# Attention phase of a graph kernel: flags made once, rotations for two chunks at a time, layer one moved by three DMAs a chunk, loads issued ahead

## The reference, cut to what matters

```python
        # attention, edge_index = (src, dst)
        q = (x @ Wq).reshape(N, N_HEADS, D_HEAD)
...
        scores = jnp.einsum('ehd,ehd->eh', q[dst], k[src]) * inv_sqrt_d
        m = jax.ops.segment_max(scores, dst, num_segments=N)
...
        e = jnp.exp(scores - m[dst])
        denom = jax.ops.segment_sum(e, dst, num_segments=N)
        msg = jax.ops.segment_sum(e[:, :, None] * v[src], dst, num_segments=N)
        attn_out = msg / jnp.maximum(denom, 1e-16)[:, :, None]
        out = attn_out.reshape(N, N_HEADS * D_HEAD) @ Wo
        return x + out
...
        # tensor product: 384 weights of an edge from its scalar, spherical harmonics Y of its direction
        R = jax.nn.relu(abs_distances[:, None] @ w1 + b1) @ w2 + b2
...
                    acc = acc + _NORM[i] * jnp.einsum('euv,ef,evi,ofi->euo', Rb[..., k], Yf, Fb, C)
...
        out = out.at[dst].add(msg)
        return out
...
    h = jnp.maximum(_layernorm(x, axis=-1), 0.0)
    x = x + _L0_gnn_ref(h, L0_gnn_Wq, L0_gnn_Wk, L0_gnn_Wv, L0_gnn_Wo, edge_index)
    h = jnp.maximum(_layernorm(x, axis=-1), 0.0)
    x = x + _L1_gnn_ref(h, edge_weight, edge_attr_3, edge_index, L1_gnn_w1, L1_gnn_b1, L1_gnn_w2, L1_gnn_b2)
    return x
```

## Time and profile before

| | |
|---|---|
| time, median of 3 runs | 8775.19 us (8774.19 to 8779.57) |
| profiled execution, first to last instruction | 10754.7 us |
| PE, DVE, ACT, POOL busy in it | 3832.9, 5399.1, 1875.2, 6468.4 us |
| attention loop, first to last gather | 317.7 to 4838.2 us |
| tensor-product loop, first to last gather | 5088.2 to 10541.2 us |
| largest group of instructions | L988, 3132 gathers, 3073.6 us busy |
| second | L534, 3132 gathers, 2992.4 us busy |

### The profile page before, as it was taken

One profiled execution on the slowest core, in us unless ns is written; L12 is line 12 of the kernel. 1 busy time (PEld: TensorE's weight loads), 2 busy tenths in 40 slices (PEclk: granted clock), 3 DMA queues, 4 the chain that ended last, 5 costly groups with the idle time before them and its releaser, 6 DMA issues. The chain is left out here.

```text
span 10754.7 us, 65813 instructions
## 1 busy us (share of the span) xinstructions
PE 3832.9 (36%) x15884; PEld 2560.9 (24%) x15884; DVE 5399.1 (50%) x8641; ACT 1875.2 (17%) x2288; POOL 6468.4 (60%) x6677
## 2 busy tenths in 40 slices
PE   1000000000000000000576666666766666676663
PEld 0000000000000000000344444444444444444442
DVE  3223333333433333333566666666666666666664
ACT  0123222222222222221011111111111111111110
POOL 6776666666666666664555555555555555555554
PEclk6555555555555555555788888888888888888887
DMA  6334334334333433432122222222222222222221
GB/s 244 84 85 100 102 96 100 93 95 100 99 101 92 101 92 97 103 96 55 41 49 51 50 51 52 49 48 51 53 48 49 51 49 51 52 50 52 49 51 32
DMA packets 417113, 797.24 MB, mean 74 GB/s; under 512 B 166622, under 2 KB 244174, under 8 KB 404798
## 3 DMA queue, kind: packets, MB, share of 16 engines
q1 hardware_dynamic: 152488, 491.52, 16.4%
q0 software_dynamic: 213216, 166.16, 9.5%
q10 hardware_dynamic: 51126, 136.22, 3.3%
HBM read 499.75 MB, written 293.61 MB: 74 GB/s over the span
## 5 line engine op out<-in xcount | busy, mean ns | idle before, releaser
L988 POOL DMA_INDIRECT feat<-scratch_h,src x3132 | 3073.6, 981 | 2422.4 <-issue 1006.7
L534 POOL DMA_INDIRECT kv<-scratch_kv,src_i x3132 | 2992.4, 955 | 1533.4 <-issue 965.7
L1221 DVE TENSOR_TENSOR prod<-psR,ops 128x384 f32<-128x384 f32 (+1 forms) x3132 | 1936.3, 682 | 1807.0 <-remote 1335.6
L1014 PE MATMUL psS<-prod,ident 128*128 128x288 f32 x7656 | 2091.5, 433 | 2.1 <-DVE prod L1221 2.1
L1003 PE MATMUL psR<-whigh,stack 128*128 128x384 f16 x3132 | 1127.5, 361 | 1634.7 <-DVE prod L1221 1493.0
L1014 PEld LDWEIGHTS psS<-prod,ident 128*128 128x128 f32 x7656 | 1582.8, 208 | 470.5 <-issue 28.3
L798 PE MATMUL psA<-ident,tail 128*36 128x128 f32 x3 | 0.8, 414 | 4578.3 <-DVEq L823 4578.3
L1004 PE MATMUL psR<-wlow,capped 128*128 128x384 f16 x3132 | 1131.4, 362 | 96.7 <-issue 93.6
L798 PEld LDWEIGHTS psA<-ident,tail 128*36 128x36 f32 x3 | 0.3, 128 | 4578.5 <-DVEq L823 4578.4
L1003 PEld LDWEIGHTS psR<-whigh,stack 128*128 128x128 f16 x3132 | 323.8, 103 | 2081.8 <-DVE prod L1221 1693.0
L641 DVE TENSOR_TENSOR sq<-attr 128x162 f32<-128x162 f32 x58 | 19.1, 329 | 1518.4 <-DMA attr<-in_attr 1039.8
(11 more groups left out here) (253 smaller groups left out, 4355.2 us busy)
## 6 DMA issues: line engine op xcount, KB each, us to landing
w_row<-in_wT SPq DMA_DIRECT2D x232, 432.0 KB
stack<-scratch_hid SPq DMA_DIRECT2D x174, 576.0 KB
scratch_state<-out ACTq DMA_DIRECT2D x58, 1080.0 KB
kv<-scratch_kv,src_i POOLq DMA_INDIRECT x3132
qin<-scratch_qexp SPq DMA_DIRECT2D x58, 864.0 KB
scratch_hid<-high SPq DMA_DIRECT2D x232, 216.0 KB
scratch_hid<-low SPq DMA_DIRECT2D x232, 216.0 KB
feat<-scratch_h,src POOLq DMA_INDIRECT x3132
```

The costliest lines, as they stand in the source:

```text
L534: nc.gpsimd.indirect_dma_start(kv[b][:, t, :], None, a["kv"], bass.IndirectOffsetOnAxis(ap=src_i[b][:, t:t + 1].bitcast(U32), axis=0)).the ...
L988: nc.gpsimd.indirect_dma_start(feat[h][:, t, :], None, a["h2"], bass.IndirectOffsetOnAxis(ap=src_i[b][:, h * PACK + t:h * PACK + t + 1].bi ...
L1014: nc.tensor.matmul(psS[:, 0:GC].rearrange("p (t c) -> p t c", c=COLS), ident[:, :], prod[r][:, :, j, :], start=(n == 0), stop=False)
L1221: v.tensor_tensor(to[:, :, :, lo:lo + n], psR[:, g % 2, :, frm:frm + n * JC].rearrange("p t (j u) -> p t j u", j=JC), ops[j % 2][:, ts, x ...
```

## The change: what it does

- **Flags.** All destination numbers are loaded at once (`dst_all`, 128x3132) before the loop, and one instruction makes all 58 chunks' flags, straight into the tile that `tensor_product` reads. In the loop L646, L648 and L650 go, with their loads; ScalarE makes the penalty from the flags by a scale and a bias.
- **Frames.** Directions are loaded, squared, rooted and turned for two chunks at a time (128x108 where 128x54 stood). The turning stands in the second chunk of a pair, after the split and before the wait for the gathered rows. Some instructions no longer wait for the one before.
- **Layer one.** The scalars of a chunk come by one DMA, the hidden units go out by two. `w_row`, `high` and `low` are one tile each of two pieces, where each piece was a tile with a semaphore.
- **Loads ahead.** Queries of the first two chunks are loaded ahead of the loop, then each two chunks ahead; the directions a pair ahead.
- **Counting.** DVE's count of its own instructions is cleared at the end of each pair, so its waits are for constants and the register instructions between them (L115) go.

```diff
-        dst_i = [sb(f"dst_i{b}", [P, T1], I32) for b in range(2)]
-        attr = [sb(f"attr{b}", [P, T, 3]) for b in range(2)]
+        dst_all = sb("dst_all", [P, SLOTS + 1], I32)
+        attr = sb("attr", [P, 2 * T, 3])
...
-        w_row = [sb(f"w_row{q}", [P, PIECE]) for q in range(2)]
+        w_row = sb("w_row", [P, 2 * PIECE])
+        high, low = sb("high", [P, 2 * PIECE], FP16), sb("low", [P, 2 * PIECE], FP16)
...
+                def load_w(chunk):
+                    sp.dma_start(w_row[:, :],
+                                 a["wT"][bass.ds(chunk * (T * P), T * P)].rearrange("(h o n) -> h o n", h=2, o=1).to_broadcast([2, HID, 2 * PIECE])
+                                 ).then_inc(w_here, 16)
+                def store_units(units_of, row):
+                    sp.dma_start(a["hid"][bass.ds(row, HID), :].rearrange("k (h n) -> h k n", h=2),
+                                 units_of[:, :]).then_inc(hid_stored, 16)
...
                 def body(i, last):
                     for b in range(2):
...
+                        chunk = i * 2 + b
+                        if not last:
+                            sp.wait_ge(q_free, chunk + 1)
+                            load_q(b, chunk * T + 2 * T)
+                        sp.wait_ge(split_done, chunk * 2 + 3)
+                        if not (last and b == 1):
+                            load_w(chunk + 1)
+                        store_units(high, chunk * P)
+                        store_units(low, chunk * P + HID)
+                    if not last:
+                        sp.wait_ge(attr_free, i + 1)
+                        load_attr(i * (2 * T) + 2 * T)
+                    sp.wait_ge(frame_ready, i + 1)
+                    sp.dma_start(a["frame"]..., frame[:, :, :]...).then_inc(frame_stored, 16)
...
-                        nc.scalar.activation(pen_c[:, :, :], spread_front(pen[:, :], HEADS), ACT.Copy).then_inc(spread_ready, 1)
+                        nc.scalar.activation(pen_c[:, :, :], spread_front(flags, HEADS), ACT.Copy, scale=BIG, bias=-BIG).then_inc(spread_ready, 1)
...
+                        act.wait_ge(w_here, i * 32 + b * 16 + 16)
                         for q in range(2):
...
+                            if q == 0:
+                                act.wait_ge(hid_stored, i * 64 + b * 32 + 32)
+                            nc.scalar.activation(high[:, cols], units, ACT.Copy).then_inc(high_ready, 1)
...
+                vec.wait_ge(dst_loaded, 32)
+                step(v.tensor_tensor(same[:, :, 1:T1], by_chunk(dst_all[:, 1:SLOTS + 1]), by_chunk(dst_all[:, 0:SLOTS]), ALU.is_equal))
...
+                        if b == 1:
+                            vec.wait_ge(rn_ready, i + 1)
+                            rotations(step, i)
...
+                    vec.sem_clear(vec_done)
```

More of the change, by code:

```diff
@@ L495, in _ @@
                     sp.dma_start(b1[half, :], a["b1"]).then_inc(w_loaded, 16)
-                load_w(0, 0)
-                load_w(1, 0)
+                load_q(0, 0)
+                load_attr(0)
+                load_w(0)
+                load_q(1, T)
                 def body(i, last):
                     for b in range(2):
[L501 to L520, removed]
@@ L633, in _ @@
                 own_block(vec)
                 with vec.Fori(0, PAIRS) as i:
-                    step = chain(vec, vec_done, base + i * (2 * steps))
+                    step = chain(vec, vec_done)
+                    vec.wait_ge(attr_loaded, i * 16 + 16)
+                    step(v.tensor_tensor(sq[:, :, :], attr[:, :, :], attr[:, :, :], ALU.mult))
+                    step(v.tensor_reduce(rn[:, :], sq[:, :, :], axis=AX.X, op=ALU.add))
+                    vec.sem_inc(rn_asked, 1)
                     for b in range(2):
@@ L647, in _ @@
-                        vec.sem_inc(dst_free, 1)
-                        step(v.tensor_scalar(pen[:, :], same[:, :], BIG, -BIG, ALU.mult, ALU.add))
-                        vec.sem_inc(flags_ready, 1)
-                        step(v.tensor_copy(k["same"][:, bass.ds(i * 2 + b, 1), :].rearrange("p c t -> p (c t)"), same[:, :]))
-                        vec.wait_ge(rn_ready, c1)
-                        step(v.reciprocal(rn[:, :], rn[:, :]))
-                        vec.wait_ge(frame_free, c1)
-                        fr = frame[b]
@@ L663, in _ @@
-                        step(v.tensor_tensor(inv[:, :], sgn[:, :], nz, ALU.add))
-                        step(v.reciprocal(inv[:, :], inv[:, :]))
-                        step(v.scalar_tensor_tensor(out=xy[:, :], in0=ny, scalar=-1.0, in1=inv[:, :], op0=ALU.mult, op1=ALU.mult))
-                        step(v.tensor_tensor(fr[:, :, 6], xy[:, :], nx, ALU.mult))
-                        step(v.tensor_tensor(xy[:, :], xy[:, :], ny, ALU.mult))
-                        step(v.tensor_tensor(fr[:, :, 7], xy[:, :], sgn[:, :], ALU.add))
@@ L669, in _ @@
-                        step(v.tensor_scalar(fr[:, :, 8], ny, -1.0, None, ALU.mult))
-                        step(v.scalar_tensor_tensor(out=fr[:, :, 5], in0=nx, scalar=-1.0, in1=sgn[:, :], op0=ALU.mult, op1=ALU.mult))
-                        step(v.tensor_tensor(fr[:, :, 4], fr[:, :, 6], sgn[:, :], ALU.mult))
-                        step(v.tensor_tensor(xy[:, :], nx, inv[:, :], ALU.mult))
-                        step(v.tensor_tensor(xy[:, :], xy[:, :], fr[:, :, 5], ALU.mult))
-                        step(v.tensor_scalar(fr[:, :, 3], xy[:, :], 1.0, None, ALU.add))
@@ L707, in _ @@
                         vec.sem_inc(sums_ready, 1)
-                    assert step.count[0] == 2 * steps, step.count[0]
+                    vec.sem_clear(vec_done)
                 vec.wait_ge(sums_copied, CHUNKS * 2 + 2)
```

124 lines of the change are left out of this document (64 added, 60 removed).

## The result

| | us (lowest to highest) | runs |
|---|---|---|
| before | 8774.69 (8758.42 to 8779.57) | 4 |
| after | 10,090.76 (10,079.21 to 10,092.04) | 4 |
| ratio | 1.15 [1.1483, 1.1516] | |

The account below looks back on a forecast made before the run. The prediction took POOL's gathers to bound a timed run's attention loop. All parts counted 0 except 3 us won on POOL's own pace: 8775.2 - 3 = 8772 us, no change that can be told (0.66); 8-in-10 range 8670 to 8800.

Parts of the forecast that it names:

- Layer one: Attention loop, SP's queue: 5 DMAs a chunk for 17, claimed 0 timed; a load at most 5.5 us later, cost 0.
- slack of 26.9 us: Attention loop, each chunk: POOL's gathers of 67.5 us less the 40.6 us chain of DVE and ACT, claimed to cover late loads.
- POOL paces a timed run of before: Attention loop: gathers at 1.25 us, 67.5 us a chunk, outlast the 40.6 us chain, so the change leaves the bound untouched.
- rival of a real stall in attention: Attention loop: up to 164 us of stalls are real when timed and go, giving 8611, middle 8693; chance 0.24.
- The residue: Whole timed run: 164 us left for both loops' stalls, 8775.2 less 8611.2 of outer stretches and back-to-back gathers.
- Stalls in the profile and hardly any in a timed run: Both gather loops: a timed run has at most 164 of the profile's 2143 us of stalls, 8%.
- The span of 10,190 in the profile: Profiled execution after the change: nearly all 567 us of POOL's buffer waits go, from 10754.7 to about 10190 (10150 to 10350).
- Flags, frames, loads ahead, 0 and -3 us: Attention loop: these parts gain 0 timed; fewer DVE instructions beside POOL's gathers win 3 us, bounds 0 and 25.
- Slower rival: Attention loop: the scalars' load has rows twice as long, gathers queue behind them, 46 us, giving 8821; chance 0.07.
- Faster, because DVE's steps hold gathers up: Attention loop: 25 fewer DVE steps a pair free POOL, 25 us (8750) or 196 us (8579); chance 0.03.
- DVE's idle goes to `kv`: Attention loop, changed kernel's profile: DVE idles ahead of the product with gathered keys, on `kv`'s landing, instead of before the squares.

Follow-up runs that it names:

- both undone: Changed kernel with its joined load made two DMAs and its two stores four, of 64 partitions each: 8793.21 us, 1.002 of before; 0.9846 on a slower chip.

## Why the prediction was wrong

The step that failed is *Layer one*: "One load is now later by what the first piece had ahead, 5.5 us at most ... Cost 0". It priced the joined DMA by the issue it saves and took its transfer at the pace that the rows of before showed for DMAs of 64 partitions. None of the rows that it read was of a DMA led by 2. The transfer's length should have been an unknown with bounds, the upper one for rows two at a time instead of sixteen. Where the prediction had the load 5.5 us later, its rows take 38.3 us and the stores' another 36.1 behind them. The wait that carries the loss in one chunk of a pair was named ("ACT's first fp16 copy of a chunk waits for all stores of the last one"); the one of the other chunk, DVE's for the directions behind the stores on SP's queue, was not. The slack of 26.9 us was the wrong measure, too: one joined set of 36 to 38 us exceeds it and costs 2.9 or 11.6 us in the whole kernel, because it runs beside DVE's and ACT's work. What counts is the turn from one load to the next. It exceeds the gathers by 88.2 - 67.5 = 20.6 us a chunk, and 58 of these are the 1195.7 (67.5 is 3917.8 / 58).

Point by point:
- *POOL paces a timed run of before.* Right: the loop is 3917.8 us against 3915 worked out, without buffer waits. So the rival of a real stall in attention, up to 164 us, had nothing to gain. The residue itself is 287 us (of the span of 8772.2) and not 164, since the outer stretches are 654.8 us and not 781.2, and nearly all of it is in the tensor product, whose gathers follow each other by 1.34 us and not 1.25.
- *Stalls in the profile and hardly any in a timed run.* Right in the numbers; but what differs is the chip, not profiling: on either pace the span is within 0.3% of the times.
- *The span of 10,190 in the profile.* Wrong. That 10,090.1 lies near it is chance: it is of a quick chip, and on the slower pace, for which the forecast was made, the span is 11,385.8. With the DMAs undone there it is 10,568.0: the loop falls to 4379.9 us; the waits are gone, but only 140.6 of their 567 us come back, since the gathers are longer there, 1.063 us in the mean against 0.955 (3132 times 0.108 is 338 us), with issue gaps of 1054.4 us against 965.7 (89 more). Why they are longer there is open.
- *Flags, frames, loads ahead, 0 and -3 us.* Right to 0.2%: with the DMAs undone the kernel is 1.002 [1.0011, 1.0029], slower and not faster. DVE is busy 170.7 us less over the whole span of after (5410.5 to 5239.7; 186 forecast), off the path.
- *Slower rival.* It named larger rows that hold the gathers up, 8821. The sign was right, the mechanism wrong: the gather's mean stayed at 945 ns, and both undone keeps rows of 13,824 bytes at 8793. (On the slower pace both undone does have gathers of 1.063 us, but there it gains.)
- *Faster, because DVE's steps hold gathers up.* Not seen: in the loop of both undone DVE runs 1368 instructions for 2091, and the gather's mean is 0.948 us against 0.946.
- *DVE's idle goes to `kv`.* Wrong for after (1511.1 us on the directions), right for both undone.

## What to carry to other kernels

When two DMAs are joined into one, write down the first dimension of each side's view: it, not the count of DMAs or the bytes, decided here whether rows went 2, 4 or 16 at a time, and the rows of two DMAs of 64 partitions took 9.0 us where those of one led by 2 took 38.3. (One DMA with the 64 in front of the 2 was not tried.) Fewer DMAs on a queue is a gain only if that queue's issue is on the path; a transfer's length is to be priced anew whenever its shape changes. Slack is spent once: sum what is in series before calling each edit free, since here each of the two edits cost 0.03 and 0.13% alone (2.9 and 11.6 us over the kernel with neither) and 15% together.

## What the hardware showed that I had not expected

A row of the same size is faster with fewer in flight: 13,824 bytes in 0.540 us with two, 0.860 with four, about 1.0 with sixteen. So leaving out 7/8 of the parallel rows makes the transfer longer by some four times (38.3 us against 9.0), not eight. DMAs of one queue that are led by 2 don't run beside each other but share the same two places, and a later DMA led by 128 has 16 of its 128 rows wait there, so that it lands only when they are done. An engine that issues behind slow transfers can be held at the issue itself: SP stood 34.32 and 50.89 us over one DMA each, and a load of 162 KB behind took 41.2 us to land where it took 12.0. And one kernel has two paces by chip, 8774 and 10,570 to 10,745 us, though in the attention loop of before a gather takes 0.944 to 0.947 us in the middle on either.
